# A graph network kernel: the degree walk unrolled, with its one-hot as the moving operand, and waits of GpSimd for walk tiles

## The reference

```python
def _sage_conv(h, src, dst, Wl, bl, Wr):            # block 0, twice
    agg = jax.ops.segment_sum(h[src], dst, num_segments=N)
    deg = jax.ops.segment_sum(jnp.ones((src.shape[0],)), dst, num_segments=N)
    return (agg / jnp.maximum(deg, 1.0)[:, None]) @ Wl.T + bl + h @ Wr.T
...
def gcn_conv(x, edge_index, W, b):                  # blocks 1 and 2, with self-loops appended
    dinv = rsqrt(deg); msg = (x @ W)[src] * (dinv[src] * dinv[dst])[:, None]
    return jax.ops.segment_sum(msg, dst, num_segments=n) + b
...
# block 3: deg = segment_sum(edge_weight, dst), w = dinv[src] * edge_weight * dinv[dst];
# in each of 3 layers 3 hops x = segment_sum(w[:, None] * x[src], dst), out += x @ W[l, k]
```

## Time and profile before

| what | value |
|---|---|
| median of 3 runs | 7355.84 us (7343.09 to 7356.77) |
| the profiled execution, its own time | 7354.22 us |
| its span, first to last instruction | 7352.4 us |
| TensorE matmul busy | 6796.8 us (92%) |
| TensorE weight load busy | 4000.4 us (54%) |
| VectorE busy | 2161.7 us (29%) |
| GpSimd busy | 4721.4 us (64%) |
| ScalarE busy | 363.9 us (5%) |
| data moved | 2083.26 MB, 283 GB/s in the mean |
| mean granted TensorE clock | 0.985 of full |

### The profile page before, as it was taken

How to read it: one execution, slowest core, us unless ns; L and a number is a source line. 1 busy time by engine, 2 the same in 40 slices (tenths; PEclk the granted TensorE clock), 3 DMA queues, 4 the chain that set the end, 5 groups by cost and what they waited for, 6 DMA issues and landing times.

```text
span 7352.4 us, 75993 instructions
## 1 busy us (share of the span) xinstructions
PE 6796.8 (92%) x25725; PEld 4000.4 (54%) x25726; DVE 2161.7 (29%) x8178; ACT 363.9 (5%) x1003; POOL 4721.4 (64%) x4931
## 2 busy tenths in 40 slices
PE   0699749999999999998999999999999999999999
PEld 0598325555555555555555555555555555555555
DVE  8444602222222111222222233222222332222244
ACT  0000000000010000000000000000000000000000
POOL 0677777677666776776647477464765747557474
PEclk9999879999999999999999999999999999999999
DMA  9877737788787887887878788787888878788887
GB/s 367 348 290 295 251 129 263 253 295 275 279 279 266 285 295 275 307 273 278 291 275 297 272 315 297 274 288 271 299 300 281 298 279 291 271 291 301 296 298 246
DMA packets 606900, 2083.26 MB, mean 283 GB/s; under 512 B 133012, under 2 KB 332599, under 8 KB 411580
## 3 DMA queue, kind: packets, MB, share of 16 engines
q1 hardware_dynamic: 332302, 1667.02, 63.2%
q0 software_dynamic: 157840, 242.67, 10.9%
q10 hardware_dynamic: 116412, 169.16, 6.3%
HBM read 1804.71 MB, written 274.95 MB: 283 GB/s over the span
## 4 chain that ended last, share of the span: by engine, by line
PE 71%; DMA 11%; issue 10%; POOL 7%; DVE 0%; SPq 0%; ACT 0%; POOLq 0%; ACTq 0%; DVEq 0%
PE pwide L1021 57%; PE pstep L1051 11%; POOL counts L591 4%; DMA counts<-lane_val,lane_idx 4%; DMA counts<-zz 2%; POOL ring_f L628 2%; PE pwide L1105 1%; DMA weights<-lane_val,lane_idx 1%; POOL weights L591 1%; DMA ring_f<-table,f_src 1%; DMA room<-weights 1%; DMA ring_f<-in_x,f_src 1%; PE pwide L1104 0%; PE pwide L1067 0%; PE pwide L1071 0%
## 5 line engine op out<-in xcount | busy, mean ns | idle before, releaser
L628 POOL DMA_INDIRECT ring_f<-table,f_src x3456 | 3287.4, 951 | 1915.5 <-issue 874.9
L1021 PE MATMUL pwide<-room,hcur 128*128 128x512 f32 (+1 forms) x6468 | 2696.6, 561 | 116.2 <-DMA room<-counts 109.3
L1021 PE MATMUL pwide<-room,acc 128*128 128x512 f32 (+1 forms) x6370 | 2654.9, 560 | 25.2 <-DMA room<-weights 23.3
L1021 PEld LDWEIGHTS pwide<-room,hcur 128*128 128x128 f32 x6468 | 1127.7, 191 | 1167.5 <-issue 1162.1
L1021 PEld LDWEIGHTS pwide<-room,acc 128*128 128x128 f32 x6370 | 1106.2, 191 | 1040.6 <-issue 1037.4
L1051 PEld LDWEIGHTS pstep<-hot,ring_f 128*128 128x128 f32 x7956 | 1092.4, 192 | 649.3 <-issue 556.1
L1537 DVE TENSOR_SCALAR hot<-iota,f_dst,f_wgt 128x128 f32<-128x128 f32 x2808 | 793.0, 361 | 1588.0 <-PE pstep L1051 1575.1
L1051 PE MATMUL pstep<-hot,ring_f 128*128 128x128 f32 x7956 | 1126.7, 277 | 85.4 <-DMA ring_f<-table,f_src 68.2
L591 POOL DMA_INDIRECT counts<-lane_val,lane_idx x660 | 648.4, 982 | 222.7 <-issue 180.5
L591 POOL DMA_INDIRECT weights<-lane_val,lane_idx x568 | 557.2, 981 | 173.1 <-issue 162.1
L1536 DVE TENSOR_SCALAR hot<-iota,f_dst 128x128 f32<-128x128 f32 x1170 | 261.8, 303 | 812.3 <-PE pstep L1051 798.6
(11 more groups left out here) (261 smaller groups left out, 1686.4 us busy)
## 6 DMA issues: line engine op xcount, KB each, us to landing
room<-weights SPq DMA_DIRECT2D x864, 1024.0 KB
room<-counts SPq DMA_DIRECT2D x540, 1024.0 KB
counts<-zz ACTq DMA_DIRECT2D x64, 1792.0 KB
weights<-zz SPq DMA_DIRECT2D x57, 1792.0 KB
ring_f<-table,f_src POOLq DMA_INDIRECT x3456
room<-weights SPq DMA_DIRECT2D x180, 256.0 KB
room<-counts SPq DMA_DIRECT2D x105, 256.0 KB
table<-acc ACTq DMA_DIRECT2D x84, 256.0 KB
```

What stands on the lines that cost most here:

```text
L628: pool.indirect_dma_start(out=ring_f[:, slot, :], out_offset=None, in_=rows_from[:, :], in_offset=bass.IndirectOffsetOnAxis(ap=f_src[:, c: ...
L1021: ins = pe.matmul(bank[:, 0:w * P], x_of(a)[:, first + o, :], room[:, n % SLOTS, o * w * P:(o + 1) * w * P], start=begins, stop=ends and n ...
```

## The change

The walk is written out tile by tile on both engines, with batches of seven one-hots in place of three. The stationary operand is now the pair of two columns and the one-hot moves, so a tile's sums are two rows of 128 in `pstep[it % 2]`, and two banks alternate. VectorE copies the rows to `degree_rows`, which lies in `room`; at the end TensorE transposes the 49 pairs of rows into `t_bank[0]` and one copy brings them to `degs`. GpSimd waits for the copies: ahead of the 159th scatter for the first tile, and so on with one tile more every eight scatters, until the 543rd and the 49th tile.

```diff
-WB = SPAN // HB
-assert SPAN % HB == 0 and SPAN <= HOTS and SPAN >= MIX + 3
+HW = 7
+WB = SPAN // HW
+assert SPAN % HW == 0 and SPAN <= HOTS and SPAN >= MIX + 3
 AHEAD_UNITS = 6
+WALK_AT, PER_TILE = 150, 8
+assert WALK_AT + PER_TILE * TILES <= LISTS[0].lane + LISTS[1].lane
...
+        degree_rows = rflat[:, 0:TILES * P].rearrange("p (t d) -> p t d", d=P)
...
                     for i in range(LISTS[which].lane):
+                        put = which * LISTS[0].lane + i - WALK_AT
+                        if put > 0 and put % PER_TILE == 0 and put // PER_TILE <= TILES:
+                            pool.wait_ge(acc_done, put // PER_TILE)
                         scatter(which, i)
...
-                pe.sem_inc(pe_step, WB)
-                with pe.Fori(0, TILES) as it:
+                for it in range(TILES):
                     for j in range(SPAN):
-                        if j == 0:
-                            pe.wait_ge(acc_done, it + 1)
-                        if j % HB == 0:
-                            pe.wait_ge(hot_ready, it * WB + (j // HB + 1))
-                        ins = pe.matmul(pstep[0][:, 0:2], hot[:, j, :],
-                                        degree_of[:, bass.ds(it * SPAN + j, 1), :].rearrange("p c a -> p (c a)"),
+                        if j == 0 and it >= 2:
+                            pe.wait_ge(acc_done, it - 1)
+                        if j % HW == 0:
+                            pe.wait_ge(hot_ready, it * WB + j // HW + 1)
+                        ins = pe.matmul(pstep[it % 2][0:2, 0:P], degree_of[:, it * SPAN + j, :], hot[:, j, :],
                                         start=j == 0, stop=j == SPAN - 1)
-                        if j % HB == HB - 1:
+                        if j % HW == HW - 1:
                             ins.then_inc(pe_step, 1)
+                pe.wait_ge(acc_done, TILES)
+                for t in range(TILES):
+                    ins = pe.transpose(t_bank[0][:, 2 * t:2 * t + 2], degree_rows[0:2, t, :], ident[0:2, 0:2])
+                ins.then_inc(p_fast, 1)
...
             def degree_walk():
-                with dve.Fori(0, TILES) as it:
-                    for b in range(WB):
-                        dve.wait_ge(pe_step, it * WB + (b + 1))
-                        for j in range(b * HB, (b + 1) * HB):
-                            ins = V.tensor_scalar(hot[:, j, :], iota[:, :], f_dst_flat[:, bass.ds(it * SPAN + j, 1)], None,
-                                                  ALU.is_equal)
-                        ins.then_inc(hot_ready, 1)
-                        if b == 1:
-                            dve.wait_ge(pe_step, it * WB + WB)
-                            V.tensor_copy(deg_sums[:, bass.ds(it, 1), :],
-                                          pstep[0][:, 0:2].rearrange("p (a d) -> p a d", a=1)).then_inc(acc_done, 1)
-                dve.wait_ge(pe_step, (TILES + 1) * WB)
-                link(V.tensor_copy(deg_sums[:, TILES, :], pstep[0][:, 0:2]))
+                for n in range(TILES * WB):
+                    it, b = divmod(n, WB)
+                    if it:
+                        dve.wait_ge(pe_step, n - WB + 1)
+                    for j in range(b * HW, (b + 1) * HW):
+                        ins = V.tensor_scalar(hot[:, j, :], iota[:, :], f_dst[:, it, j:j + 1], None, ALU.is_equal)
+                    ins.then_inc(hot_ready, 1)
+                    if it and b == 1:
+                        dve.wait_ge(pe_step, it * WB)
+                        V.tensor_copy(degree_rows[0:2, it - 1, :], pstep[(it - 1) % 2][0:2, 0:P]).then_inc(acc_done, 1)
+                dve.wait_ge(pe_step, TILES * WB)
+                V.tensor_copy(degree_rows[0:2, TILES - 1, :], pstep[(TILES - 1) % 2][0:2, 0:P]).then_inc(acc_done, 1)
+                dve.wait_ge(p_fast, 2)
+                link(V.tensor_copy(degs, t_bank[0][:, 0:2 * TILES].rearrange("p (t a) -> p t a", a=2)))
```

More of the change, by code:

```diff
@@ L250, in program @@
         f_dst = sb("f_dst", [P, TILES, SPAN])
-        f_dst_flat = f_dst[:, :, :].rearrange("p t c -> p (t c)")
         begun = sb("begun", [P, NS + 1])
```

## The result

The changed kernel takes 7376.48 us (median of 7 runs, 7372.68 to 7389.34) against 7355.84 us for the kernel before (7 runs, 7343.09 to 7366.14): ratio 1.0031, 95% interval 1.002 to 1.0043. The prediction, 7353 us and at most 7371, was wrong. The profiled execution took 7385.11 us. An execution that ran disturbed, at a longer time than the others of its kernel, is left out of all times and ratios here.

A forecast was written before the change was run, and what follows sets the result against it. GpSimd's back-to-back scatters and gathers were taken to bound the opening, with the walk off the path. All terms were zero except 1.4 us gained from list 2: 7354.2 - 1.4 = about 7353 us, range 7333 to 7371.

The forecast's parts named there:

- VectorE against GpSimd: Scatters beside the walk's builds: excess stays 8 us as builds stay 1029, taken as zero; bounds 8 us either way.
- Rival 1: 190 scatters beside the walk each wait for one build, 0.203 us: excess 39 us, 7384 us; chance 0.07.
- The waits on GpSimd: 49 waits ahead of the 159th to 543rd scatter: already satisfied, taken as zero, upper bound 2.8 us.
- The early start: Behind the walk: TensorE finishes five groups 45 us earlier, then waits that much longer for list 1; worth zero.
- Two columns, one-hot moving: Degree walk: a tile takes 4.9 us instead of 9.69, walk ends at about 494 us; zero on the path.
- List 2's arithmetic: VectorE's arithmetic moves away from the first unit loads, speeding 20 scatters: 1.4 us gained, bounds nothing and 8 us.
- Contention fades: Scatters beside walk and list 2's arithmetic: both 8 us excesses vanish, 7338 us; chance 0.08.

The follow-up runs named there:

- the third chip: The changed kernel, unedited, run again on a chip of the first kind against the kernel before (7355.58 us there): 7379.18 us, ratio 1.0035.

## Why the prediction was wrong, step by step

**The step that failed** is the term "VectorE against GpSimd", taken as zero because the builds stay 1029, with 8 us of loss as its upper bound. The walk's excess went from 8 us to 23 (25.5 in the trace of the third chip, 185.33 us for 167 scatters), a loss of 15 to 18. The reasoning counted builds. They did stay harmless: without the copies beside them the kernel is at 7359 us, inside the range. What I left out of this term is the one VectorE instruction whose form the change altered. I priced the copy at the 0.16 us of the old one and only as part of a tile's length, off the path. It takes VectorE 0.28 us, which costs nothing on the path, and it costs GpSimd up to 0.9 us at about half of the scatters that start near it.

**Rival 1**, *VectorE starves GpSimd*, had the place and the sign. Its price per scatter was 0.203 us, one build, for all 190, from 0.12 us on; measured were 0.137 us in the mean, but made of 25 scatters of 1.5 to 1.85 us and of others that take 1.016 us in the mean, 0.04 more than before. Its mechanism, each scatter waiting for one build of a dense train, was not what happened. The Trainium skill (SBUF — State Buffer, "Who interferes with whom") says that the two engines exclude each other "for the whole instruction". If a scatter asks for the ports once, that gives at most one build, 0.28 us; a scatter of 2.92 us beside 14 builds is held seven times that. The measurement decides: behind such a copy GpSimd is held for many builds in a row, by what mechanism isn't shown.

**The waits on GpSimd** at zero: right on the chips of the first kind (7354.57 us with them in the kernel before; in the changed kernel's trace GpSimd never waited for VectorE's copies). The prediction's "each later one gains 0.5 us of lead" is a slip: 168 us at the first and 210 at the last make 42 / 48 = 0.9 us; nothing hangs on it. On the other chips the waits alone bring as much as the whole change, which no row of before could have shown.

**The early start** was worth nothing, as said. Loads came at 741 us, not 724, since the last zeroing DMAs of `weights` went out at 732.60 instead of 714.47; in other traces of changed kernels too (735.31, 732.61), and I didn't follow it up, as it is off the path. SyncE waited 163.7 us for list 1 (about 150 predicted) and TensorE stood idle 151 us (141). The granted clock in that wait was 0.50 (0.51 before); the lower of the two levels (1.2 GHz) cost nothing, by the equal 6266 us behind it.

**Two columns, one-hot moving**: a tile took 4.59 us instead of 4.9, because VectorE is the bound and not TensorE; the walk's last copy came at 491.4 instead of 494.

**List 2's arithmetic**, moved away from the unit loads, was to give 1.4 us. Beside it the 192 scatters between 500 and 750 us are 189.56 - 192 x 0.957 = 5.8 us over, in place of some 8: a gain of 2, as far as one trace tells.

**Contention fades** (rival 3) was not to be had in full. With the iota in PSUM all scatters of the span together are 5.0 us over 0.957 each, in the kernel before 16.8. Yet from the first to the last scatter it is only 5.0 us less (864.8 against 869.8), and the time is the same. From 760 to 860 us a scatter came every 1.38 us instead of 1.37, though each took 0.957 instead of 1.026: the gaps in which GpSimd waits for its data to land grew, beside loads that now fill the DMA engines (share 0.90 of that stretch instead of 0.67 in the earlier trace rows).

## What to carry to other kernels

When VectorE works beside indirect DMAs that bound the kernel, list every form of VectorE instruction that the change alters, the rare ones too, and look at what the indirect DMAs near each do; means over a stretch hide 25 bad cases among 170. The cure here is to move the copy to ScalarE or to let the builds read PSUM (7359.35 and 7356.19 us), but neither beats the kernel before where it takes 7356 us. And a result can hang on the chip: look at what the kernel before takes on it.

## What the runs showed that was not expected

- A 2x128 copy from PSUM to SBUF in front of builds that read SBUF keeps GpSimd's scatter from ending until many builds have passed: it takes 1.3 to 1.85 us with one copy a tile, up to 2.92 us with two, 0.95 us when the builds read PSUM. A 128x2 copy in the same place doesn't. With one copy a tile (first kind of chip) every held scatter ends 1.49 to 2.37 us behind the start of the copy, beside the seventh, eighth or eleventh build, while the builds go on starting about 0.2 us apart; a break of the train is thus not what ends these. With two copies 28 of the 65 held ones end beside a break, the one behind the 14th build. What ends a hold stays open. Whether the two partitions, the 128 elements or the 0.28 us of the copy bring it about was not tried.
- Two kinds of chip: 7356 us and 8935 to 9004 us for the same kernel. On the second, while scatters follow one another without a pause, TensorE does 104 matmul records in 300 us and GpSimd's semaphore instructions take up to 1.4 us instead of at most 0.043. Short pauses of GpSimd end that: 49 waits gained 416 us in the kernel before (8518.89 against 8935.25) and 195 in the changed one (8544.78 against 8739.86). Why issue is slow there stays open. So does the rest of the distance between the chips: late in the run they differ too, with no scatters about.

```profile
5000.00:5500.00 500.00, 496.89 (x1915) 282.72 (x1914) 128.12 (x433) 25.35 (x72) 308.91 (x326) 1.00 0.83 290
```
```profile
5000.00:5500.00 500.00, 466.40 (x1661) 256.45 (x1660) 144.28 (x545) 24.59 (x71) 282.49 (x297) 0.95 0.72 266
```

The first row is the kernel before on a chip of the first kind, the second the kernel before with the waits on one of the second. They aren't at the same point of the program, but the work per 500 us is about a tenth less there: 1661 matmul records instead of 1915, 266 GB/s instead of 290.
- On chips of the second kind batches of three builds (8500.52 us, 0.9499) and the kernel before with the waits (8518.89 us, 0.9516) came out best; their intervals overlap, so neither is shown to beat the other.
